# Attention units regrouped: from one head by 512 tokens to two heads by 256 tokens, late and early halves in turn

## The reference, cut to what matters

```python
x = x + 0.5 * ffn(layernorm(x), ...)
x = x + attn(layernorm(x), wq, wk, wv, wo, key_weights)
x = x + 0.5 * ffn(layernorm(x), ...)
...
# attn: x is (4, 512, 256); 16 query heads, 4 key/value heads, head size 128
q, k, v = x @ wq.T, x @ wk.T, x @ wv.T      # split into heads
q, k = apply_rope(q), apply_rope(k)
k = k * key_weights[None, :, None, None]
scores = einsum('bhqd,bhkd->bhqk', q, k) * 128 ** -0.5
scores = where(causal, -inf, scores)
out = einsum('bhqk,bhkd->bhqd', softmax(scores), v)
return out.reshape(B, S, 2048) @ wo.T
```

## Time and profile before

| | us |
|---|---|
| median of 3 runs | 825.73 (825.53 to 825.89) |
| the profiled execution | 827.23 |
| its span in the profile | 825.4 |
| mean granted TensorE clock | 0.989 of full speed |

### The profile page before, as it was taken

How to read it: one execution, slowest core, us unless ns; L and a number is a source line. 1 busy time by engine, 2 the same in 40 slices (tenths; PEclk the granted TensorE clock), 3 DMA queues, 4 the chain that set the end, 5 groups by cost and what they waited for, 6 DMA issues and landing times.

```text
span 825.4 us, 16046 instructions
## 1 busy us (share of the span) xinstructions
PE 791.6 (96%) x4712; PEld 697.2 (84%) x4712; DVE 655.1 (79%) x1917; ACT 507.4 (61%) x1250; POOL 517.5 (63%) x408
## 2 busy tenths in 40 slices
PE   7899999869999999999999999999999999999996
PEld 4688887758999989999899998999999988788885
DVE  6888996897678686786876868768687799988876
ACT  3555665657667576676865767557676586344543
POOL 4545739965878778777777777877878761112302
PEclk9999999979999999999999999999999999999998
DMA  9245321201132122212311313122131110000001
GB/s 290 82 144 191 120 85 39 66 13 39 27 77 76 38 51 76 51 27 62 105 28 45 93 30 80 29 85 51 35 92 25 39 27 1 1 1 26 2 26 52
DMA packets 28998, 50.09 MB, mean 61 GB/s; under 512 B 3874, under 2 KB 9634, under 8 KB 28962
## 3 DMA queue, kind: packets, MB, share of 16 engines
q1 hardware_dynamic: 28964, 49.67, 21.5%
HBM read 18.72 MB, written 9.96 MB: 35 GB/s over the span
## 4 chain that ended last, share of the span: by engine, by line
PE 80%; DVE 10%; ACT 3%; issue 2%; POOL 2%; DMA 1%; SPq 1%; POOLq 0%; DVEq 0%; ACTq 0%
PE pt L1713 8%; PE pj L1648 5%; PE pj L1650 5%; PE pj L1649 5%; PE o L1727 5%; PE o L1728 4%; PE o L1729 4%; PE sc L1702 4%; PE sc L1701 4%; PE sc L1700 4%; PE pj L1757 4%; PE pj L1758 3%; PE pj L1759 3%; PE sc L983 3%; PE sc L984 3%; PE sc L985 3%
## 5 line engine op out<-in xcount | busy, mean ns | idle before, releaser
L1273 POOL TENSOR_TENSOR at_ql<-at_rot,at_qh 128x512 fp32r<-128x512 f32 x64 | 82.6, 1291 | 100.5 <-ACT at_qh L1502 100.4
L1549 ACT ACTIVATE at_pth<-pt 128x512 fp32r<-128x512 f32 (+1 forms) x192 | 94.0, 524 | 82.4 <-PE pt L1713 82.4
L1400 DVE TENSOR_TENSOR at_ptl<-pt,at_pth 128x512 fp32r<-128x512 f32 (+1 forms) x192 | 108.9, 594 | 44.9 <-ACT at_pth L1549 44.7
L1543 ACT ACTIVATE at_pr<-at_pr,at_low 128x512 f32<-128x512 f32 (+3 forms) x256 | 140.5, 557 | 4.4 <-DVE at_low L1386 4.2
L1395 DVE TENSOR_SCALAR at_pr<-at_pr,at_inv 128x128 f32<-128x128 f32 (+3 forms) x256 | 107.6, 482 | 2.3
L1285 POOL TENSOR_TENSOR at_rot<-at_rot,gc 128x512 f32<-128x512 f32 x80 | 103.3, 1291 | 6.3
L1281 POOL TENSOR_TENSOR at_rot<-ga,cos 128x512 f32<-128x512 f32 x80 | 103.9, 1298 | 2.4 <-POOL at_ql L1273 2.3
L1283 POOL TENSOR_TENSOR gc<-gc,sin 128x512 f32<-128x512 f32 x80 | 103.7, 1296 | 1.0 <-DMA gc<-ga 1.0
L1713 PE MATMUL pt<-ident,at_pr 128*128 128x128 f32 x640 | 93.5, 277 | 8.3 <-DVE at_ptl L1400 4.6
L1386 DVE CUSTOM_DVE_ANT_0 at_pr<-sc,at_mask 128x512 f32<-128x512 f32 (+2 forms) x192 | 100.7, 548 | 0.2
L1502 ACT ACTIVATE at_qh<-at_rot 128x512 fp32r<-128x512 f32 x64 | 40.6, 634 | 91.1 <-POOL at_rot L1285 91.1
(11 more groups left out here) (286 smaller groups left out, 2265.2 us busy)
## 6 DMA issues: line engine op xcount, KB each, us to landing
gc<-ga SPq DMA_DIRECT2D x160, 128.0 KB, 2.3
ga<-in_attn_w SPq DMA_DIRECT2D x8, 384.0 KB, 4.9
gb<-attn_split SPq DMA_DIRECT2D x6, 512.0 KB, 4.1
at_wo<-attn_split SPq DMA_DIRECT2D x6, 512.0 KB, 4.0
attn_split<-gb SPq DMA_DIRECT2D x6, 384.0 KB, 2.4
attn_split<-gc SPq DMA_DIRECT2D x6, 384.0 KB, 3.3
x<-in_x SPq DMA_DIRECT2D x4, 512.0 KB, 9.5
e_raw<-in_expert_w SPq DMA_DIRECT2D x8, 256.0 KB, 6.6
```

What stands on the lines that cost most here:

```text
L1400: dve.tensor_tensor(ptl[h % 2][:, cols], pt[(NF * h + k) % 2][:, 0:FLEN[k]], pth[h % 2][:, cols].bitcast(F32), ALU.subtract).then_inc(lo_d ...
L1543: act.activation(pr[h % 2][:, cols], pr[h % 2][:, cols], ACT.Exp, bias=low[h % 2][:, i:i + 1], scale=-1.0, accum_out=tot[h % 2][:, i:i + 1 ...
```

## The change

Still four units a step, but a unit is two heads (a pair) by 256 tokens: u = 0 is pair 0, late tokens (256 to 511); u = 1 is pair 0, early tokens; u = 2 and u = 3 the same for pair 1. The stationary tile of the scores holds 64 queries of both heads. A chunk c (1 to 8) of 64 queries needs 64 c keys: a late unit streams 512, 448, 384 and 320 columns, an early one 256, 192, 128 and 64. A late unit has 14 transposes in four fills and `weigh` streams 512, 512, 512 and 256 columns; an early unit has 6 transposes in two fills, and 512 and 256 columns.

The passes are kept, with other contents. The projections of step s + 1 or s + 2 and the two halves of `output` of step s - 1 are spread anew over the four passes, and Q1 is now projected two steps ahead with K and Q0. The scores of a pair need both of its queries: `scores` now waits for rest 2 (pair 0) or rest 4 (pair 1). On ACT lead 0 moves between the exponentials of pass 0, and leads 1 to 4 come just ahead of `out_lead` in passes 0 to 3. POOL's order is not changed. The rows of Q are written with the two heads interleaved every 64 columns; the weight loads of a group come in three pairs of DMAs instead of two, the last behind a wait for `vt_done`. The diff, cut to its core:

```diff
+        CHUNKS = ((8, 7, 6, 5), (4, 3, 2, 1))
+        FLEN = ((4 * P, 4 * P, 4 * P, 2 * P), (4 * P, 2 * P))
...
-        q_hi, q_lo = [sb("qh0", [P, 2, SEQ], F32R)], [sb("ql0", [P, 2, SEQ], F32R)]
+        q_hi, q_lo = [sb("qh0", [P, 2 * BT, 2, QC], F32R)], [sb("ql0", [P, 2 * BT, 2, QC], F32R)]
...
-        PLACE = {3: (0, 0), 2: (1, 0), 1: (2, 0), 0: (2, 2 * P)}
+        PLACE = {8: (0, 0), 7: (1, 0), 6: (2, 0), 5: (0, 0), 4: (1, 0), 3: (1, 2 * P), 2: (2, 0), 1: (2, P)}
...
 # sync
+                    if r == 2 and new_proj is not None:
+                        load_proj(new_proj, [w[:, :, 0:HD] for w in wb], SECOND, wq_in)
...
                     if r == NR - 1 and new_proj is not None:
-                        load_proj(new_proj, wb, LATER, wb_in)
+                        sp.wait_ge(vt_done, s + 1).then_inc(passed, 1)
+                        load_proj(new_proj, [w[:, :, HD:4 * HD] for w in wb], LATER, wb_in)
...
 # scalar, step
                     if more2:
-                        exps(n + 2, h2, QT[:2])
-                    if h == 0 and ahead:
-                        if not first:
-                            raw_out(s + 1, 2)
-                        value_out(s + 1)
+                        exps(s2, u2, range(2))
+                    if u == 0 and ahead:
+                        rotated_lead(act, s + 1, 0)
                     if more2:
-                        exps(n + 2, h2, QT[2:])
+                        exps(s2, u2, range(2, BT))
...
+                    elif not first and u in (1, 2) and ahead:
+                        raw_out(s + 1, u + 2)
+                    if u == (1 if first else 2) and ahead:
+                        value_out(s + 1)
...
-                    if h == 0 and ahead:
-                        rotated_lead(act, s + 1, 0)
-                    if h == 0 and ahead and not first:
-                        rotated_lead(act, s + 1, 1)
-                    if more1:
-                        prob_lead(n + 1, h1, 2)
-                    out_lead(n, s, h)
-                    if h > 0 and ahead:
-                        rotated_lead(act, s + 1, h + 1)
-                    if h == G - 1 and ahead:
+                    if ahead:
+                        rotated_lead(act, s + 1, u + 1)
+                    out_lead(s, u)
+                    if u == UNITS - 1 and ahead == 2:
+                        raw_out(s + 2, 2)
+                    if u == UNITS - 1 and ahead:
                         value_lead(s + 1)
...
+                    if u % 2 and more1:
+                        prob_lead(s1, u1, 2)
+                        prob_lead(s1, u1, 3)
...
 # tensor
-            def scores(n, s, h):
-                pe.wait_ge(ql_done, NR * s + h + 2)
+            def scores(s, u, places=range(BT)):
+                kind, pair = u % 2, u // 2
+                before = BT * unit(s, u) - 2 * BT
...
+                    if k == 0:
+                        pe.wait_ge(ql_done, NR * s + 2 * pair + 3)
+                    if kind == 0:
+                        if begun or k == 3:
+                            pe.wait_ge(mx_done, before + (4, 6, 8, 9)[k])
+                    elif c % 2 == 0:
+                        pe.wait_ge(mx_done, before + (6 if c == 4 else 7))
+                    hi, lo = (q[pair][:, c - 1].rearrange("p h q -> p (h q)") for q in (q_hi, q_lo))
...
 # tensor, step
                     if more2:
-                        scores(n + 2, s if h + 2 < G else s + 1, h2)
+                        scores(s2, u2, range(3) if u2 % 2 == 0 else range(BT))
                     if more1:
-                        transpose_p(n + 1, h1, (0, 1))
...
+                        transpose_p(s1, u1, (0, 1))
+                    if more2 and u2 % 2 == 0:
+                        scores(s2, u2, (3,))
+                    if u == 0 and not first:
+                        output_late(s - 1)
...
+                    if u == 1 and not first:
                         if ahead:
+                            query(s + 1, 2)
+                        output_early(s - 1, not ahead)
+                    if u == 2 and ahead and not first:
+                        query(s + 1, 3)
+                        value(s + 1)
+                    if u == UNITS - 1 and ahead == 2:
                         key(s + 2)
                         query(s + 2, 0)
...
+                    weigh(s, u)
+                    if u == UNITS - 1 and ahead == 2:
+                        query(s + 2, 1)
+                    if u == UNITS - 1 and ahead:
                         value_T(s + 1, ahead == 2)
-                    if more1:
-                        transpose_p(n + 1, h1, (2,))
+                    if u % 2 and more1:
+                        transpose_p(s1, u1, (2, 3))
```

More of the change, by code:

```diff
@@ L1401, in prob_rest, with out_rest @@
                                   ALU.subtract).then_inc(lo_done, 1)
[L1403 to L1406, removed]
+            def out_rest(s, u):
+                lead, rest = out_parts(u)
+                dve.wait_ge(oh_done, unit(s, u) + 1)
+                dve.tensor_tensor(rest, o_heads, lead.bitcast(F32), ALU.subtract).then_inc(ol_done, 1)
@@ L1450, in step @@
-                    if first and h == 0:
-                        rows_final(last_block)
[L1452 to L1455, removed]
+                        rows_final(last_block)
+                    if u < 2 and not first:
+                        add_output(s - 1, 1 - u)
+                    if last and u == 2:
+                        add_last(0)
+                    out_rest(s, u)
@@ L1493, in vector @@
             last_pairs()
-            add_output(STEPS - 1, part=1)
+            add_last(2)
         def rows_normed(pool):
@@ new lines, in exps, with prob_lead @@
+            def exps(s, u, places=range(BT)):
+                kind = u % 2
+                for k in places:
+                    act.wait_ge(mx_done, BT * unit(s, u) + k + 1)
+                    a = pr[kind][:, columns(CHUNKS[kind][k])]
+                    act.activation(a, a, ACT.Exp, bias=low[kind][:, k:k + 1],
+                                   scale=-1.0, accum_out=tot[kind][:, k:k + 1]).then_inc(ex_done, 1)
+            def prob_lead(s, u, k):
+                kind = u % 2
+                act.wait_ge(pt_ready, fill(s, u, k) + 1)
+                cols = slice(k * SEQ, k * SEQ + FLEN[kind][k])
+                act.activation(pth[kind][:, cols], pt[k % 2][:, 0:FLEN[kind][k]], ACT.Copy).then_inc(hi_done, 1)
@@ L1555, in step, with out_lead @@
+            def out_lead(s, u):
+                act.wait_ge(o_ready, unit(s, u) + 1)
+                act.activation(out_parts(u)[0], o_heads, ACT.Copy).then_inc(oh_done, 1)
             def step(s, first, ahead):
-                for h in range(G):
-                    n = G * s + h
-                    h1, h2 = (h + 1) % G, (h + 2) % G
-                    more1, more2 = ahead or h + 1 < G, ahead or h + 2 < G
+                for u in range(UNITS):
+                    s1, u1 = following(s, u, 1)
+                    s2, u2 = following(s, u, 2)
+                    more1, more2 = ahead or u + 1 < UNITS, ahead or u + 2 < UNITS
@@ L1597, in step @@
                         act.activation(first_pair(gb, wa_all)[0], e_raw[:, 0:2, :], ACT.Copy).then_inc(early, 1)
-                    if not ahead and h == 2:
+                    if not ahead and u == 2:
                         z_lead(*NORMS[2])
@@ new lines, in output @@
+                for t in range(2):
+                    tok = slice((2 * half + t) * P, (2 * half + t + 1) * P)
+                    o = bank[:, t * D:(t + 1) * D]
+                    for h in heads:
+                        pe.matmul(o, oh[:, h, tok], wo[0][:, h, :], start=(h == heads[0]), stop=False)
+                        pe.matmul(o, oh[:, h, tok], wo[1][:, h, :], start=False, stop=False)
+                        r = pe.matmul(o, ol[:, h, tok], wo[0][:, h, :], start=False, stop=(h == heads[-1]))
@@ L1788, in step @@
+                    if u == 2 and ahead and not first:
+                        query(s + 1, 3)
+                        value(s + 1)
+                    if u == UNITS - 1 and ahead == 2:
                         key(s + 2)
                         query(s + 2, 0)
-                    elif h == G - 1 and not ahead:
-                        output(s, range(G - 1), (0,))
-                    weigh(n, s, h)
-                    if h == G - 1 and not ahead:
-                        pe.wait_ge(zlo_done, C * len(NORMS))
-                        router()
@@ L1796, in step @@
-                    if h == G - 1 and not ahead:
-                        output(s, range(G - 1), (1,))
-                    if h == G - 1 and ahead:
-                        value_T(s + 1, ahead == 2)
-                    if more1:
-                        transpose_p(n + 1, h1, (2,))
-                    if first and h in (1, 2):
-                        transpose_z(*NORMS[h - 1])
-                    if not ahead and h == 2:
+                    if u == 2 and not ahead:
```

(3 more changed lines are left out.)

526 lines of the change are left out of this document (264 added, 262 removed).

## The result

| | before | after |
|---|---|---|
| median of 4 runs, us | 825.81 (825.53 to 825.91) | 863.11 (861.93 to 864.01) |
| profiled execution: time / span, us | 827.23 / 825.4 | 861.93 / 860.1 |
| mean granted clock | 0.989 | 0.976 |

Ratio 1.0449, 95% interval 1.0436 to 1.0462: 37 us slower. The prediction was 871 in a range of 838 to 888.

What follows compares the result with a forecast made beforehand. PE bounds the kernel before; after, the POOL-ACT hand-over chain to rest 2 makes PE wait. Loop 23, clock 18, step 14 2.9, step 15 -1.0, start 2: 45 on 827.2 gives 872, 871 on the median's scale; range 838 to 888.

Steps and rivals of the forecast that it cites:

- PE's own work: In the loop, fewer score and weigh columns and fewer switches save PE 1.1 us of 33.9 a step.
- PE stays the bound: Rival: rest 2 comes in time, PE never waits in the loop, and the change wins, 811 us; chance 9%.
- The moved wait: At the head of pass 2 PE idles 2.8 us until rest 2 ends at 19.2; steps 35.7 us, +23 over 13.
- may not be done when pass 1 or 3 wants its transposes: Rival part: DVE's normalise, for 1664 columns instead of 1280, comes late; in the longer-chain case, 886 us, chance 11%.
- a wait of PE mainly for DVE: Sign named in advance that would show the forecast wrong, in PE's waits; no size given.
- The clock: After PE's idling the clock falls to its lower level, 1.2 us a step; 13 steps and two gaps, +18.
- the clock holds: Rival: the hand-over chain binds the loop but the clock does not fall, 853 us; chance 27%.
- The edges: Outside the loop: step 14 +2.9, step 15 -1.0, start +2 because first scores wait for rest 2.
- the late rest 4: In step 14's short pass 3, rest 4 comes late behind V's copy; part of that step's +2.9 us.
- ACT's two waits for the rotary sums: Sign that the forecast is right: ACT waits twice for the rotary sums, in passes 0 and 1.
- the mean clock: Sign that the forecast is right: a granted clock below 0.97.
- The strided rests: POOL's writes of Q in runs of 64 columns: taken as 0, up to 0.66 us a step in the range.

Runs made afterwards that it cites:

- Experiment 7: Changed kernel with normalise also summing its rows and POOL's order pipelined (rotate 1 while ACT makes lead 0, and so on): 816.56 us, ratio 0.9887.
- experiment 8: Kernel before, with normalise also summing its rows and POOL's order pipelined, as a control: 825.92 us beside 826.02, ratio 0.9997.
- experiment 1: Changed kernel with the normalise multiplication written as multiply, add 0.0, with the row's sum thrown away: 868.28 us, ratio 1.0486.
- (3): Changed kernel with lead 0 on ACT moved behind all four exponentials of pass 0 instead of two, except in the first step: 903.18 us, ratio 1.092.
- experiment 2: Changed kernel with POOL's order in the loop pipelined, turning the next vector while ACT makes the lead of the last: 861.5 us, ratio 1.0412.
- experiment 5: Changed kernel with six thrown-away matmuls of 512 columns in PE's wait for normalise in pass 1: 862.56 us, ratio 1.0442.
- experiment 4: Kernel of experiment 1 with nine thrown-away matmuls of 512 columns in PE's wait before pass 2's first scores: 854.73 us, ratio 1.0342.

## Why the prediction was right

**PE's own work**, 1.1 us less a step, 32.8: right. Experiment 7, where PE never waits, shows 32.74 against 33.90, and experiment 8 that nothing else in it is a gain. Of the rivals, "PE stays the bound" (811) is thus what the change comes near once its waits are taken away (816.56); the kernel itself went the other way.

**The moved wait**, 19.2 us to rest 2 and steps of 35.7: right in its size, 19.0 and, in nine steps of 13, 35.64. That rest 2 is what decides in those is shown from three sides: take PE's other wait away and the whole wait returns at rest 2 (experiment 1), make the chain 1.1 us longer and the step follows (3), shorten it and that wait alone goes (2). Its place on PE was wrong: the 2.8 us of idling at the head of pass 2 became 1.71 us in pass 1 and 0.85 there. The step that failed is that `normalise` was costed at nothing on the path and left to a rival ("may not be done when pass 1 or 3 wants its transposes"). It runs beside POOL's rotate 1, at 4.55 us. The sign given for a failed forecast, "a wait of PE mainly for DVE", did appear (23.8 us against 9.4) and was a bad sign: of two waits in series the first takes the idle time to its name, and the second decides. Only with the second gone does the first bind (experiment 2).

**The clock**, 18 us: the mechanism right, the term mis-sized for this kernel. Some 2 us of it are in the loop (experiment 5). A single wait at the head of pass 2, as the forecast had it, is experiment 1, with 2.41 us for 2.8: there the falls cost 1.6 us in 9 of 13 steps, 1.1 a step for the 1.2 taken. The split wait spared it twice over: a wait of 1.71 us was followed by a fall in 4 steps only, and the time lost then lay ahead of the wait for rest 2. That "the clock holds" (853) was nearer in the loop. The price itself rested on one fall: the wait of 2.17 us of the earlier trace rows is there in all 12 profiled executions, at 2.12 to 2.18 us, and only in that of the kernel before has the clock fallen behind it.

**The edges**, +3.9 without the clock: too low, +9.8. The start took 5.5 for 2, and these hide more: PE's first projection of attention begins at 125.24 us in the profiled execution of the kernel before and at 123.25 in that of the kernel after, so from there to the end of step 0 the start grew from 76.5 to 84.0 us, by 7.5. Of the regrouped kernels those without the form of experiment 1 take 84.0 to 84.5 us for this stretch, those with it 79.9 to 81.1: so 3 to 4 us of it are `normalise` once more, and not the hand-over to rest 2, which the term was made of. But that form shortens the start of the kernel before as well, by 1.1 to 75.4 (experiment 8). Between the two kernels that have it, 75.4 and 80.7 (experiment 7), some 5 us remain, and what they are stays open. At the end the prediction put the late rest 4 into step 14; it falls into step 15, as a wait of 1.74 us, and PE also waits 2.50 us there for DVE's `prob_rest`, with no projection left to work on meanwhile. On the timeline of PE:

```profile
708.23 0.50 PE L1756 MATMUL sc<-at_keys,at_qh 128*128 128x512 f32 x1 [1.74 <-POOL at_ql L1295]
...
727.42 0.85 PE L1771 MATMUL pt<-ident,at_pr 128*128 128x128 f32 x6 [2.50 <-DVE at_ptl L1433]
```

So the total was 8 us too high on the medians (10 on the profiled executions), since two errors went opposite ways: 16 us too much for the clock, 6 too little for the edges. That they cancel in part is luck. Of the signs, ACT's two waits for the rotary sums came (4.65 and 0.88 us), and the mean clock stayed at 0.976, above the 0.97 that was named.

The strided rests (0.66 a step kept in the range) cost nothing: the rests of queries take 1.27 to 1.31 us, as in the earlier trace rows, and rest 0 takes 1.29 for 1.61.

## What to carry to other kernels

Two waits of one engine, one behind the other, hide each other: each looks removable in the waits view, and removing either alone gives nothing. Before a change that makes an engine wait, list everything that it will want in the same stretch, and judge what a wait is worth by making the next one visible. In these runs a wait of TensorE cost its length and, where the clock fell and no later wait covered it, the speed behind it (1.6 us in nine steps of experiment 1).

## What was not expected of the hardware

The four fp32 multiplications of 1664 columns took 1.48 us alone, 4.55 to 4.97 beside POOL's back-to-back operations, and 2.36 in a form that also sums its rows, whatever POOL did. POOL's own two operations beside the plain form took 1.47 and 1.43 us instead of 1.28 and 1.30. The Trainium skill (SBUF — State Buffer, Who interferes with whom) says that such an operation of VectorE can take a pair of ports that it shares with GpSimd, that then each holds the pair for its whole length while the other waits, and that the form that writes its accumulator does not take that pair. These rows agree: one by one, the four multiplications of the step at 385.96 end at 394.14, 395.53, 396.89 and 398.20 us, the last three some 0.2 us behind the ends of POOL's operations at 395.28, 396.68 and 398.02.

Useless work made a kernel 1.4% faster (experiment 4). By these runs PE's longest wait in a step and the falls behind it go together: 1.71 us, 4 of 13 steps; 2.07, 6; 2.41, 9; 3.10, all 13, in four of them for twice as long.
